# Router columns as weights in a ViT tower kernel: 512 positions stream, the logits are transposed afterwards

## The chip, the core and the metric

The kernel runs on one core of a Trainium2 chip. The metric is the device time of one execution in microseconds (us), from the first to the last instruction with what lies around it. Five engines work side by side: PE (TensorE, matrix products), DVE (VectorE), ACT (ScalarE), POOL (GpSimd) and SP (SyncE, which issues transfers). Each runs its own list in order and waits on semaphores for the others.

## What is computed

Four images pass through a tokenizer, a linear attention layer and a mixture of experts. Cut to what matters here:

```python
h = tokenizer(x)                        # sin and cos of 6 bands, 6912 features -> 192, 512 tokens per image
h = concat([cls_tok, h])
h = h + attention(layernorm(h))
x = layernorm(h)                        # input of the feed-forward part
probs = softmax(x @ router_w)           # 192 -> 8 experts
gates, idx = top_k(probs, 2)
gates = gates / sum(gates)
g = silu(einsum('bsd,edh->bseh', x, w_gate)); u = einsum('bsd,edh->bseh', x, w_up)
routed = sum over experts of dense_g * ((g * u) @ w_down)
shared = silu(x @ ws_gate) * (x @ ws_up) @ ws_down
alpha = sigmoid(x @ sg_w + sg_b)
out = h + alpha * shared + (1 - alpha) * routed
```

The router here is the product of the 192 features of a token with 10 columns: 8 experts, one column for alpha, one of zeros.

## The kernel before

Everything is in float32. Where exactness to float32 is wanted at the faster matmul format fp32r, an operand is split into a high part and a rest, and the products of the parts are summed in PSUM: high times high, high times rest, rest times high, and for the last 64 features (stacked twice, as `wrb`) two products.

The work has three stages. First come four records b = 0 to 3, one for each image. Each has nine projections `project(b, k)` of 24 matmuls (6 feature groups i times 4 blocks of 128 tokens), and the features of a projection are made beforehand by POOL (`rounds`), DVE (`remainders`) and ACT (`sines`, two of them). Between the projections stand the steps `attn1` to `attn8` of the attention of the record before; index a counts them, a = 0 for the class tokens and a = b for the image before record b. The second stage is the chunks q = 0 to 18 of the shared expert (`up(q)`: ten matmuls of 512 columns, `silu`, `hidden`, `down(q)`), between which the attention of the last image (a = 4) stands, and the splitting of the routed experts' weights into high part and rest (`expert_hi` on ACT, `expert_lo` on DVE). The third is 39 tiles of 128 routed rows, the remaining chunks and the sum.

All orders are written by hand, engine by engine; the numbers Q_... say at which chunk a step stands. The router runs five times. For a = 0 it stands between projections 7 and 8 of record 0; for a = 1 and 2 in records 2 and 3, behind `attn1(b)` and before `project(b, 1)`; for a = 3 before chunk 0; for a = 4 after chunk 11. On PE (L1430 to L1444) it takes, for each block of 128 tokens, the token features as weights (128 columns) and streams the 10 router columns, in five matmuls:

```python
o, c = ps[0:TP, logit_bank(a), 16 * i:16 * i + NR], slice(i * P, i * P + TP)
pe.matmul(o, xh_a_[:, c], wra_hi[:, :], start=True, stop=False)
```

The logits land with tokens on partitions, and DVE's `router(a)` copies them (L929) and picks the two best experts in a chain of some 14 short steps, then `ranks` on PE counts how many tokens each expert has, `places` on DVE works out the slots, and POOL scatters the tokens to them (`scatter`, L433). ACT's `router(a)` (L571) is one exponent for the gates, which DVE's `gates(a)` takes. SP loads the routed experts' weights (`raw_a`, `raw_b`) after the last projection, their down weights (`wd_ea`, `wd_eb`, L353 and L354) when all weights are split, and the first tiles `xs` (L363) when all tokens are scattered. `finish(f)` on DVE (L1044) empties the PSUM bank of the shared expert of an image; `down` of the next image's first chunk waits for it.

In records 2 and 3 the order on ACT is: `sines(b, 1)`, `sines(b, 2)`, `attn1(b)` (the copy `xt_a`, L496), `router(b - 1)`, `sines(b, 3)`.

## Time and profile before

| what | value |
|---|---|
| median of 3 runs | 570.83 us (570.6 to 571.26) |
| the profiled execution | 570.71 us |
| its span, first to last instruction | 568.9 us |
| mean granted clock of TensorE | 0.994 of full speed |
| DVE busy | 363.0 us (64%) |
| ACT busy | 245.9 us (43%) |
| POOL busy | 174.0 us (31%) |

The profile is one execution, recorded by the hardware. Its page gives busy times by engine, its other views the single instructions in order of time, what each engine waited for, and the clock that TensorE was granted. Matmul records overlap their neighbours, so the distance from start to start is what one costs, not the length of a record. A float32 matmul shows as two records, so 24 matmuls are x48; the fp32r ones and transposes show as one.

### The profile page before, as it was taken

Reading aid. Unit: us, or ns where it says so; the run is one execution under the profiler, and the core shown is the slowest. Engines: PE = TensorE matmul, PEld = TensorE weight load, DVE = VectorE, ACT = ScalarE, POOL = GpSimd, SP = SyncE. Lnnn points to the kernel's source line nnn. Section 1 sums busy time; section 2 is a strip of 40 time slices with the busy share of each in tenths; the row PEclk is TensorE's granted clock in tenths of the full one; section 3 lists DMA queues with packets and bytes.
Section 4 is the critical chain, followed back from the end, with each engine's and each line's share of the span. In section 5 each row is a group of like instructions: output and inputs, shape, how many; then the busy total and the mean of one; then the engine's idle time right before and its main releaser. Section 6 shows DMA issues by size and latency. Waiting matters only on the chain.

```text
span 568.9 us, 9027 instructions
## 1 busy us (share of the span) xinstructions
PE 555.4 (98%) x3247; PEld 510.8 (90%) x3247; DVE 363.0 (64%) x1040; ACT 245.9 (43%) x343; POOL 174.0 (31%) x200
## 2 busy tenths in 40 slices
PE   5999999999999999999999999999999999999997
PEld 5998999799999989999979899977888889999965
DVE  7736787532968736779761787376787546666537
ACT  3465364654225753442575523254224134545410
POOL 6413133122225311674311461001300504454410
PEclk9998999999999999999999999999998999999999
DMA  8900067000000000210000010330100561531164
GB/s 330 323 21 20 3 216 243 20 10 20 20 18 20 20 0 11 75 56 1 1 0 10 20 37 20 98 126 23 62 2 1 185 206 54 164 95 52 55 199 152
DMA packets 23487, 42.48 MB, mean 75 GB/s; under 512 B 2502, under 2 KB 15044, under 8 KB 23348
## 3 DMA queue, kind: packets, MB, share of 16 engines
q1 hardware_dynamic: 19560, 33.31, 18.1%
q0 software_dynamic: 3472, 8.07, 4.0%
q10 hardware_dynamic: 412, 0.53, 0.4%
q8 instruction: 27, 0.44, 0.3%
q14 instruction: 16, 0.13, 0.1%
HBM read 31.74 MB, written 14.79 MB: 82 GB/s over the span
## 4 chain that ended last, share of the span: by engine, by line
PE 90%; DVE 5%; ACT 3%; DMA 1%; issue 1%; POOL 0%; ACTq 0%; DVEq 0%
PE ps L1312 47%; PE ps L1505 4%; PE ps L1391 2%; PE ps L1557 2%; PE ps L1559 2%; PE ps L1467 2%; PE ps L1469 2%; PE ps L1470 2%; PE ps L1468 2%; PE ps L1471 2%; PE ps L1368 2%; PE ps L1535 1%; PE ps L1537 1%; PE ps L1536 1%; PE ps L1539 1%; PE ps L1538 1%
## 5 line engine op out<-in xcount | busy, mean ns | idle before, releaser
L1312 PE MATMUL ps<-w_tok,feat 128*128 128x192 f32 x1728 | 292.0, 330 | 7.5 <-ACT feat L469 6.3
L1312 PEld LDWEIGHTS ps<-w_tok,feat 128*128 128x128 f32 x1728 | 284.0, 192 | 11.0 <-issue 10.6
L403 POOL TENSOR_SCALAR feat<-fx 128x512 int32<-128x512 f32 x108 | 93.2, 878 | 204.7 <-PE ps L1312 201.3
L478 ACT ACTIVATE feat<-feat 128x1536 f32<-128x1536 f32 x35 | 51.9, 1484 | 118.6 <-DVE feat L773 116.0
L769 DVE SCALAR_TENSOR_TENSOR feat<-fx,feat 128x512 f32<-128x512 f32 x105 | 76.6, 782 | 1.9 <-POOL feat L403 1.5
L481 ACT ACTIVATE feat<-feat,half_pi 128x1536 f32<-128x1536 f32 x35 | 54.6, 1561 | 0.0
L439 POOL DMA_INDIRECT ydram<-yr,xs x39 | 37.4, 959 | 54.9 <-DVE yr L1085 54.9
L433 POOL DMA_INDIRECT slots<-pay_a,posi x17 | 18.4, 1082 | 74.2 <-DVE posi L1012 70.8
L773 DVE TENSOR_SCALAR feat<-feat 128x1536 int32<-128x1536 int32 x35 | 37.5, 1070 | 1.2
L1505 PE MATMUL ps<-w_down,hid_ring 128*128 128x192 f32 x192 | 36.4, 334 | 0.8 <-issue 0.4
L585 ACT ACTIVATE s_ring<-ps 128x512 f32<-128x512 f32 x24 | 14.4, 599 | 52.1 <-PE ps L1471 52.1
L1505 PEld LDWEIGHTS ps<-w_down,hid_ring 128*128 128x128 f32 x192 | 32.1, 192 | 3.0 <-issue 1.7
L1036 DVE TENSOR_TENSOR hid_ring<-s_ring,ps 128x512 f32<-128x512 f32 x24 | 16.4, 685 | 18.6 <-PE ps L1471 15.7
L607 ACT ACTIVATE xhr<-ps 128x256 fp32r<-128x256 f32 x39 | 15.0, 384 | 22.6 <-PE ps L1518 22.6
L1078 DVE TENSOR_TENSOR hidt<-sr,ps 128x192 f32<-128x192 f32 x39 | 13.8, 353 | 15.7 <-ACT sr L613 14.1
L1071 DVE TENSOR_TENSOR xlr<-ps,xhr 128x256 fp32r<-128x256 f32 x39 | 16.5, 424 | 10.6 <-ACT xhr L607 10.6
L817 DVE TENSOR_TENSOR_SCAN r<-one,s_c,r 128x512 f32<-128x512 f32 x4 | 5.1, 1284 | 27.4 <-ACT r L523 27.4
L1467 PE MATMUL ps<-X,wa_hi 128*128 128x512 f32 x48 | 22.3, 465 | 0.2 <-ACT s_ring L585 0.2
L1085 DVE TENSOR_SCALAR yr<-ps,xs 128x192 f32<-128x192 f32 x39 | 16.3, 418 | 8.6 <-PE ps L1559 8.0
L613 ACT ACTIVATE sr<-ps 128x192 f32<-128x192 f32 x39 | 12.9, 330 | 20.2 <-issue 15.4
L1557 PE MATMUL ps<-wd_ea,htr 128*128 x78 | 19.2, 328 | 0.7 <-DVE yr L1085 0.7
L1470 PE MATMUL ps<-X,wb 128*128 128x512 f32 x48 | 19.2, 400 | 0.0
(277 smaller groups left out, 857.2 us busy)
## 6 DMA issues: line engine op xcount, KB each, us to landing
slots<-in_blank SPq DMA_DIRECT2D x1, 5031.0 KB, 18.7
w_tok<-in_wT SPq DMA_DIRECT2D x7, 576.0 KB, 8.8
fx<-in_xT SPq DMA_DIRECT2D x15, 256.0 KB, 2.7
xs<-slots SPq DMA_DIRECT2D x5, 645.0 KB, 6.9
yin<-ydram SPq DMA_DIRECT2D x8, 384.0 KB, 7.2
raw_a<-in_wea SPq DMA_DIRECT2D x4, 384.0 KB, 5.1
raw_b<-in_web SPq DMA_DIRECT2D x4, 384.0 KB, 5.9
w_tok<-in_wT SPq DMA_DIRECT2D x4, 288.0 KB, 7.6
```

What stands on the lines that cost most here:

```text
L403: ins = pool.tensor_scalar(feat[:, k % SLOTS, i, :].bitcast(I32), x[:, x_block(k), :], f_col[:, fi:fi + 1], 1.0, ALU.mult, ALU.mult)
L433: pool.indirect_dma_start(slots, bass.IndirectOffsetOnAxis(ap=idx, axis=0), (pay_a[a % 2], pay_b)[c][0:TP, t, :], None).then_inc(scat, 16)
L439: pool.indirect_dma_start(ydram, bass.IndirectOffsetOnAxis(ap=idx, axis=0), yr[:, s % NYR, :], None).then_inc(yscat[s % NYR], 16)
L478: act.activation(feat[:, k % SLOTS, 0:3, :], feat[:, k % SLOTS, 0:3, :], ACT.Sin, scale=TWO_PI).then_inc(sin_ready, 1)
L481: act.activation(feat[:, k % SLOTS, 3:6, :], feat[:, k % SLOTS, 3:6, :], ACT.Sin, bias=half_pi[:, :], scale=-TWO_PI).then_inc(sin_ready, 1)
L769: ins = dve.scalar_tensor_tensor(feat[:, s, i, :], x[:, x_block(k), :], f_col[:, fi:fi + 1], feat[:, s, i, :].bitcast(I32), ALU.mult, ALU. ...
L773: dve.tensor_scalar(feat[:, s, 3:6, :].bitcast(I32), feat[:, s, 0:3, :].bitcast(I32), 0x7FFFFFFF, None, ALU.bitwise_and).then_inc(r_ready, 1)
L1312: ins = pe.matmul(ps[:, TOK[a % 2][t // 2], (t % 2) * D:(t % 2 + 1) * D], feat[:, k % SLOTS, i, t * P:(t + 1) * P], w_tok[:, k, i, :], sta ...
L1467: pe.matmul(o, wa_hi[:, c, i, :], xh, start=True, stop=False)
L1470: pe.matmul(o, wb[:, c, i, :], yh, start=False, stop=False)
L1505: ins = pe.matmul(ps[:, DN0 + t // 2, (t % 2) * D:(t % 2 + 1) * D], hid_ring[:, q % 3, t * P:(t + 1) * P], w_down[:, c, :], start=(c == 0 ...
L1557: pe.matmul(o, htr[:, s % 2, 0:P], wd_ea[:, bass.ds(e, 1), :].rearrange("p e n -> p (e n)"), start=True, stop=False)
```

## The change

The operands of the router change sides. The router's columns become the weights, high part and rest side by side in one tile `wra` of 20 columns (and `wrb` of 10), and 512 token positions stream past them: four matmuls in place of twenty, with the logits transposed in PSUM, 20 rows by 512. ACT copies them to SBUF (`take_lt`, into the new tile `lt`), PE transposes them back block by block (`router_rows`), and DVE's first step adds the two halves instead of copying.

On PE `router_rows` stands later than `router`: in records 2 and 3 after the first sixth of `project(b, 1)`, in record 0 after half of `project(0, 8)`, for a = 3 after `up(0)`, for a = 4 after `down(9)`. On ACT `take_lt(b - 1)` stands behind `attn1(b)`, and the exponent of `router(b - 1)` moves behind `sines(b, 3)`.

The split of the routed weights goes from quarters to eighths and stands at chunks 4, 4, 4, 7, 7, 9, 10, 10 on ACT (5, 5, 5, 8, 8, 10, 11, 11 on DVE) where it stood at 4, 7, 10, 13 (5, 8, 11, 14). Their loading stays in quarters.

```diff
-EP = 4
+EL = 4
+EP = 8
-Q_HI = (4, 7, 10, 13)
-Q_LO = (5, 8, 11, 14)
+Q_HI = (4, 4, 4, 7, 7, 9, 10, 10)
+Q_LO = (5, 5, 5, 8, 8, 10, 11, 11)
...
-        wra_hi, wra_lo, wrb = (sb(n, [P, NR], F32R) for n in ("wra_hi", "wra_lo", "wrb"))
+        wra, wrb = sb("wra", [P, 2 * NR], F32R), sb("wrb", [P, NR], F32R)
+        lt = sb("lt", [2 * NR, T])
...
+            def take_lt(a):
+                W, TP, nt = width(a)
+                act.wait_ge(lt_psum, a + 1)
+                act.activation(lt[:, 0:W], ps[0:2 * NR, logit_bank(a), 0:W], ACT.Copy).then_inc(lt_ready, 1)
...
             sines(0, 8)
+            take_lt(0)
             sines(1, 0)
...
                 attn1(b)
                 if b >= 2:
+                    take_lt(b - 1)
+                sines(b, 3)
+                if b >= 2:
                     router(b - 1)
-                sines(b, 3)
...
+            take_lt(B - 1)
             for q in range(NQB):
...
                 if q == Q_LG:
+                    take_lt(B)
                     router(B)
...
-                next_(dve.tensor_copy(lg[0:TP, 0:nt, :], ps[0:TP, logit_bank(a), 0:16 * nt].rearrange(
-                    "p (t n) -> p t n", n=16)[:, :, 0:NE + 1]))
+                halves = ps[0:TP, logit_bank(a), 0:32 * nt].rearrange("p (t c) -> p t c", c=32)[:, :, 0:2 * NR]
+                next_(dve.tensor_reduce(lg[0:TP, 0:nt, :], halves.rearrange("p t (h n) -> p t n h", h=2)[:, :, 0:NE + 1, :],
+                                        AX_X, ALU.add))
...
+                o = ps[0:2 * NR, logit_bank(a), 0:W]
+                pe.matmul(o, wra[:, :], xh_a_, start=True, stop=False, skip_group_check=True)
+                pe.matmul(o, wra[:, :], xl_a_, start=False, stop=False, skip_group_check=True)
+                pe.matmul(o[0:NR], wrb[:, :], xh_b_, start=False, stop=False, skip_group_check=True)
+                pe.matmul(o[0:NR], wrb[:, :], xl_b_, start=False, stop=True, skip_group_check=True).then_inc(lt_psum, 1)
+
+            def router_rows(a):
+                W, TP, nt = width(a)
+                pe.wait_ge(lt_ready, a + 1)
                 for i in range(nt):
...
+                    ins = pe.transpose(ps[0:TP, logit_bank(a), 32 * i:32 * i + 2 * NR], lt[:, i * P:i * P + TP],
+                                       ident[0:2 * NR, 0:2 * NR])
                 ins.then_inc(lg_psum, 1)
...
             router(0)
-            project(0, 8)
+            project(0, 8, range(3))
+            router_rows(0)
+            project(0, 8, range(3, 6))
...
                     router(b - 1)
-                project(b, 1)
+                project(b, 1, range(1))
+                if b >= 2:
+                    router_rows(b - 1)
+                project(b, 1, range(1, 6))
...
                 up(q)
+                if q == 0:
+                    router_rows(B - 1)
...
                     down(q - 2)
+                if q == Q_LG:
+                    router_rows(B)
```

How the rows stand on PE in record 2, around the router of a = 1, before (`xn` is the normalized input of the attention, `X` the split tokens, `feat` and `w_tok` the features and weights of the projection):

```order
L1323 MATMUL ps<-pack,xn 128x128 x4
L1325 MATMUL ps<-pack,xn 64x128 x4
L1439 MATMUL ps<-wra_hi,X 128x10
L1440 MATMUL ps<-wra_lo,X 128x10
L1441 MATMUL ps<-wra_hi,X 128x10
L1442 MATMUL ps<-wrb,X 128x10
L1443 MATMUL ps<-wrb,X 128x10
...
L1312 MATMUL ps<-w_tok,feat 128x192 x24
L1349 MATMUL ps<-xt_a,pack 128x512
```

The five router rows stand four times. The same place on PE after the change:

```order
L1339 MATMUL ps<-pack,xn 128x128 x4
L1341 MATMUL ps<-pack,xn 64x128 x4
L1456 MATMUL ps<-X,wra 20x512
L1457 MATMUL ps<-X,wra 20x512
L1458 MATMUL ps<-X,wrb 10x512
L1459 MATMUL ps<-X,wrb 10x512
L1327 MATMUL ps<-w_tok,feat 128x192 x4
L1465 MATMUL ps<-pack,lt 128x20 x4
L1327 MATMUL ps<-w_tok,feat 128x192 x20
L1365 MATMUL ps<-xt_a,pack 128x512
```

Four wide rows replace the twenty, and the transposes stand behind 4 of the projection's 24 matmuls. On ACT in the same record, from `sines(2, 2)` on, before:

```order
L478 ACTIVATE feat<-feat 128x1536
L481 ACTIVATE feat<-feat,half_pi 128x1536
L496 ACTIVATE xt_a<-ps 128x512
L571 ACT_TABLE_LOAD
L571 ACTIVATE ez<-dz 128x8
L478 ACT_TABLE_LOAD
L478 ACTIVATE feat<-feat 128x1536
L481 ACTIVATE feat<-feat,half_pi 128x1536
L515 ACT_TABLE_LOAD
L515 ACTIVATE r<-ps,pack 128x512
```

The first two rows are `sines(2, 2)`, the seventh and eighth `sines(2, 3)`. And after the change:

```order
L480 ACTIVATE feat<-feat 128x1536
L483 ACTIVATE feat<-feat,half_pi 128x1536
L498 ACTIVATE xt_a<-ps 128x512
L573 ACTIVATE lt<-ps 20x512
L480 ACTIVATE feat<-feat 128x1536
L483 ACTIVATE feat<-feat,half_pi 128x1536
L578 ACT_TABLE_LOAD
L578 ACTIVATE ez<-dz 128x8
L517 ACTIVATE r<-ps,pack 128x512
```

The copy `lt` stands behind `xt_a`, the exponent behind `sines(2, 3)`, and two loads of a function table are gone. On DVE at chunks 10 and 11, before (`X` is the split of the last image's tokens, L929 the start of its router):

```order
L909 TENSOR_TENSOR X<-ps,X 128x512
L910 TENSOR_TENSOR X<-ps,X 128x512
L1036 TENSOR_TENSOR hid_ring<-s_ring,ps 128x512
L1060 TENSOR_TENSOR e_lo<-raw_a,e_hi 128x768
L1064 TENSOR_TENSOR e_b<-raw_b,e_b 64x768
L929 COPY lg<-ps 128x36
```

And after the change:

```order
L1074 TENSOR_TENSOR e_lo<-raw_a,e_hi 128x384
L1078 TENSOR_TENSOR e_b<-raw_b,e_b 64x384
L922 TENSOR_TENSOR X<-ps,X 128x512
L923 TENSOR_TENSOR X<-ps,X 128x512
L1050 TENSOR_TENSOR hid_ring<-s_ring,ps 128x512
L1074 TENSOR_TENSOR e_lo<-raw_a,e_hi 128x384
L1078 TENSOR_TENSOR e_b<-raw_b,e_b 64x384
L1074 TENSOR_TENSOR e_lo<-raw_a,e_hi 128x384
L1078 TENSOR_TENSOR e_b<-raw_b,e_b 64x384
L943 TENSOR_REDUCE lg<-ps 128x36
```

The same amount of split stands ahead of the router's first step, one more eighth ahead of the token split.

## Rows read from the trace of the kernel before

**Rows 1.** The page, busy time by engine: us, share of the span, instructions.
```profile
PE 555.4 (98%) x3247; PEld 510.8 (90%) x3247; DVE 363.0 (64%) x1040; ACT 245.9 (43%) x343; POOL 174.0 (31%) x200
```

**Rows 2.** What PE waited for: total us, times, longest.
```profile
PE ps L1312 <- ACT feat L469: 6.3, 1, 6.3
```

**Rows 3.** Timeline of PE, records 2 and 3: start, us, work (copies).
```profile
186.78 0.25 PE L1439 MATMUL ps<-wra_hi,X 128*128 128x10 f32 x1
...
189.01 8.05 PE L1312 MATMUL ps<-w_tok,feat 128*128 128x192 f32 x48
196.90 0.59 PE L1349 MATMUL ps<-xt_a,pack 128*128 128x512 f32 x1
...
282.07 8.05 PE L1312 MATMUL ps<-w_tok,feat 128*128 128x192 f32 x48
```

**Rows 4.** Timeline of ACT, records 2 and 3; in brackets the idle time before.
```profile
187.91 1.48 ACT L478 ACTIVATE feat<-feat 128x1536 f32<-128x1536 f32 x1 [5.81 <-DVE feat L773]
189.30 1.56 ACT L481 ACTIVATE feat<-feat,half_pi 128x1536 f32<-128x1536 f32 x1
190.76 0.57 ACT L496 ACTIVATE xt_a<-ps 128x512 f32<-128x512 f32 x1
...
283.83 0.58 ACT L496 ACTIVATE xt_a<-ps 128x512 f32<-128x512 f32 x1
```

**Rows 5.** Timeline of DVE, before record 1 and in record 2.
```profile
88.53 1.14 DVE L739 BATCH_NORM_STATS2 st<-H 128x6 f32<-128x192 f32 x4 [2.42 <-ACT H L489]
...
92.50 1.25 DVE L755 TENSOR_SCALAR xn<-H,mv,y 128x192 f32<-128x192 f32 x4
...
200.92 0.69 DVE L804 TENSOR_SCALAR r<-ps 128x512 f32<-128x512 f32 x1 [4.71 <-PE ps L1352]
```

**Rows 6.** Timeline of PE, start of record 1.
```profile
95.23 0.60 PE L1323 MATMUL ps<-pack,xn 128*128 128x128 f32 x4
```

**Rows 7.** Timeline of PE near the end: two-column weights with 512 streaming, small transposes.
```profile
545.94 0.39 PE L1577 MATMUL ps<-wb,xc 128*2 128x512 f32 x1
546.17 0.40 PE L1467 MATMUL ps<-X,wa_hi 128*128 128x512 f32 x1
...
549.90 0.53 PE L1582 MATMUL ps<-pack,v 2*128 2x2 f32 x6
```

**Rows 8.** Timeline of PE, record 0: little work, a wait, a projection.
```profile
34.14 8.07 PE L1312 MATMUL ps<-w_tok,feat 128*128 128x192 f32 x48
...
42.86 0.48 PE L1391 MATMUL ps<-v,r 2*2 2x193 f32 x2
44.41 9.72 PE L1312 MATMUL ps<-w_tok,feat 128*128 128x192 f32 x48 [1.07 <-ACT feat L478]
```

**Rows 9.** Stretches: PE, PEld, DVE, ACT, POOL busy (instructions), PEclk, DMA, GB/s.
```profile
44.40:46.00 1.60, 1.59 (x6) 1.60 (x7) 1.33 (x9) 1.33 (x1) 0.24 (x1) 0.61 0.04 10
...
429.80:432.00 2.20, 2.20 (x11) 2.20 (x11) 1.94 (x8) 0.00 (x0) 0.00 (x0) 0.65 0.00 0
```

**Rows 10.** Timeline of PE, shared-expert chunks 1 to 12.
```profile
371.22 0.60 PE L1323 MATMUL ps<-pack,xn 128*128 128x128 f32 x4
...
429.83 2.31 PE L1505 MATMUL ps<-w_down,hid_ring 128*128 128x192 f32 x8
...
442.70 1.46 PE L1505 MATMUL ps<-w_down,hid_ring 128*128 128x192 f32 x8
```

**Rows 11.** Timeline of DVE, layer norm, weight split, router chain, finish.
```profile
369.39 1.25 DVE L755 TENSOR_SCALAR xn<-H,mv,y 128x192 f32<-128x192 f32 x4
...
398.13 0.95 DVE L1064 TENSOR_TENSOR e_b<-raw_b,e_b 64x768 fp32r<-64x768 f32 x1
400.93 0.23 DVE L859 TENSOR_SCALAR den<-ps 128x2 f32<-128x2 f32 x2 [1.85 <-PE ps L1391]
...
430.44 0.20 DVE L929 COPY lg<-ps 128x36 f32<-128x36 f32 x1
...
440.76 1.39 DVE L1044 SCALAR_TENSOR_TENSOR H<-ps,alpha,H 128x192 f32<-128x192 f32 x4
```

More of the change, by code:

```diff
@@ L201, in build @@
             xpose2 nta_ready ntb_ready wo_psum h2_ready xn2_ready xpose3 xh_ready xl_ready
-            lg_psum top_step dz_ready ez_ready gt_step oh_ready gates_ready rank_psum rk_ready pos_step slots_ready emap_ready
+            lt_psum lt_ready lg_psum top_step dz_ready ez_ready gt_step oh_ready gates_ready rank_psum rk_ready pos_step slots_ready emap_ready
             payb_ready scat
@@ L215, in build @@
          xpose2, nta_ready, ntb_ready, wo_psum, h2_ready, xn2_ready, xpose3, xh_ready, xl_ready,
-         lg_psum, top_step, dz_ready, ez_ready, gt_step, oh_ready, gates_ready, rank_psum, rk_ready, pos_step, slots_ready, emap_ready,
+         lt_psum, lt_ready, lg_psum, top_step, dz_ready, ez_ready, gt_step, oh_ready, gates_ready, rank_psum, rk_ready, pos_step, slots_ready, emap_ready,
          payb_ready, scat,
@@ L346, in _ @@
             sp.wait_ge(tok_group, NG * B)
-            for p in range(EP):
-                cut = slice(p * NE // EP, (p + 1) * NE // EP)
+            for p in range(EL):
+                cut = slice(p * NE // EL, (p + 1) * NE // EL)
                 cols = slice(cut.start * 2 * D, cut.stop * 2 * D)
@@ L595, in expert_hi @@
             def expert_hi(p):
-                act.wait_ge(eraw_in, 32 * EP)
+                act.wait_ge(eraw_in, 32 * EL)
                 cut = slice(p * NE // EP, (p + 1) * NE // EP)
@@ L703, in _ @@
                     take_ranks(B)
-                if q in Q_HI:
-                    expert_hi(Q_HI.index(q))
+                for p in range(EP):
+                    if Q_HI[p] == q:
+                        expert_hi(p)
             for i in range(NTILE + 2):
@@ L1148, in _ @@
             attn1(0)
-            dve.tensor_copy(wra_hi[:, :], wr_raw[:, 0, :])
+            dve.tensor_copy(wra[:, 0:NR], wr_raw[:, 0, :])
             dve.tensor_copy(wrb[:, :], wr_raw[:, 1, :]).then_inc(router_split, 1)
             dve.wait_ge(router_split, 1)
-            dve.tensor_tensor(wra_lo[:, :], wr_raw[:, 0, :], wra_hi[:, :].bitcast(F32), ALU.subtract)
+            dve.tensor_tensor(wra[:, NR:2 * NR], wr_raw[:, 0, :], wra[:, 0:NR].bitcast(F32), ALU.subtract)
             dve.tensor_tensor(wrb[DB:P, :], wr_raw[DB:P, 1, :], wrb[DB:P, :].bitcast(F32),
@@ L1248, in _ @@
                     places(B, [2])
-                if q in Q_LO:
-                    expert_lo(Q_LO.index(q))
+                for p in range(EP):
+                    if Q_LO[p] == q:
+                        expert_lo(p)
             dve.memset(hidt[:, :, D:2 * P], 0.0).then_inc(hidt_zero, 1)
@@ L1291, in _, with project @@
         def _(pe):
-            def project(a, k):
+            def project(a, k, recs=range(6)):
                 q = NG * a + k
@@ L1300, in project @@
                     pe.wait_ge(h_ready, a - 1)
-                for i in range(6):
+                for i in recs:
                     if q == 0 and i < 2:
@@ L1315, in project @@
                                         skip_group_check=True)
-                ins.then_inc(tok_group, 1)
+                if 5 in recs:
+                    ins.then_inc(tok_group, 1)
             def attn1(a):
@@ L1436, in router @@
                     pe.wait_ge(dz_ready, a)
-                for i in range(nt):
-                    o, c = ps[0:TP, logit_bank(a), 16 * i:16 * i + NR], slice(i * P, i * P + TP)
-                    pe.matmul(o, xh_a_[:, c], wra_hi[:, :], start=True, stop=False)
-                    pe.matmul(o, xh_a_[:, c], wra_lo[:, :], start=False, stop=False)
-                    pe.matmul(o, xl_a_[:, c], wra_hi[:, :], start=False, stop=False)
-                    pe.matmul(o, xh_b_[:, c], wrb[:, :], start=False, stop=False)
-                    ins = pe.matmul(o, xl_b_[:, c], wrb[:, :], start=False, stop=True)
+                if a >= 2:
+                    pe.wait_ge(rk_ready, a - 1)
+                o = ps[0:2 * NR, logit_bank(a), 0:W]
[6 more added lines that the diff above has]
+                pe.wait_ge(lt_ready, a + 1)
+                for i in range(nt):
+                    ins = pe.transpose(ps[0:TP, logit_bank(a), 32 * i:32 * i + 2 * NR], lt[:, i * P:i * P + TP],
+                                       ident[0:2 * NR, 0:2 * NR])
                 ins.then_inc(lg_psum, 1)
```

## The prediction

> **What bounds the kernel now.** I read the busy times by engine first: PE is busy 555.4 us of a span of 568.9 us [rows 1]. Then the list of what PE waited for: its longest entry, 6.3 us, is the start, before the first features exist [rows 2]. So nearly every microsecond that the change adds to PE's stream, or makes PE wait in it, is a microsecond of the span, and the other engines matter where PE waits for them. The timelines then show the places that the change touches: records 2 and 3 of the tokenizer, and the shared-expert chunks that run beside the last record's attention.
>
> In record 2 PE starts the router at 186.78 and the next projection at 189.01, and that projection's successor starts at 196.90 [rows 3]. Record 3 is the same 93.06 us later (282.07 for 189.01). What the reader must see beside it is ACT: at 187.91 and 189.30 it begins two sines of 1.5 us each, whose input DVE had just delivered, and only at 190.76 the copy xt_a, done at 191.33; in record 3 at 283.83 [rows 4]. ACT is thus more than 2 us behind PE's router here. Nobody minds before, since PE needs xt_a only at 196.90.
>
> **The router's arithmetic.** Now 20 matmuls with 10 streaming columns take 189.01 - 186.78 = 2.23 us, 0.11 us each, although they stream almost nothing: the 128-column weight load sets that pace. After, four matmuls stream 512 columns. The nearest rows are the class-token products, two-column weights with 512 streaming: 545.94 to 546.17, 0.23 us each [rows 7]. Four are 0.93 us. The four transposes that follow have no exact row. Six small transposes take 0.53 us [rows 7], 0.09 us each, so 0.35 us for four; at the old router's 0.11 us they would be 0.45 us, and I take that end, since the new ones load 128 columns as the router did. A router then costs 1.38 us, 0.85 us less (0.95 us with the lower end). Four routers have this form, so the work saved is 3.4 us. The router of the class tokens (two columns) stays near zero.
>
> **Does the narrow output cost a change of array mode?** The rows say no: the last two-column product starts at 545.94 and the next matmul, with 128 weight columns, 0.23 us later, the pace of the stream [rows 7]. The Trainium skill (TensorEngine Tiling, Key Properties) says that changing the tiling mode drains TensorE, which speaks against outputs of 20 and 10 columns if they switched it; by the 0.39 us that a product lasts against its 0.23 us pace, an estimate of that page's drain would be 0.16 us at each end of a router, 1.3 us for four. The trace shows none at the same kind of boundary, so I add nothing.
>
> **The wait that the change adds.** The new copy take_lt stands on ACT behind both sines and xt_a. It begins when xt_a is done, 191.33, and takes what a 512-column copy takes, 0.57 us [rows 4]: the logits are in SBUF at 191.90. PE meanwhile does the four wide matmuls from 186.78, to 187.71, and the first sixth of the projection. Its 24 matmuls took 196.90 - 189.01 = 7.89 us [rows 3], 0.33 us each, so four take 1.31 us and PE arrives at the transposes at 189.02. It waits there 2.9 us. Behind the transposes are queued the other 20 matmuls of the projection (6.58 us) and everything else on PE. The successor starts at 191.90 + 0.45 + 6.58 = 198.93 instead of 196.90: 2.0 us later. With the cheaper transposes and copies that overlap slightly it is 1.85 us; I take 1.95 us. Record 3 has the same distances (ACT 283.83, PE 282.07), so again 1.95 us. **Two records: +3.9 us.** PE waits for nothing else in these records, so nothing takes it up later.
>
> What hangs on the late logits? DVE's router starts 3.3 us later and ACT's exponent now comes behind the next two sines. DVE gates before it takes the keys at 200.92, where it had waited 4.71 us [rows 5]. The logits are 3.3 us late, the two sines cost 3.0 us [rows 4], an exponent's table load and the rest about as much as before; of these 6.3 us, 4.71 us are slack and 1.95 us come from PE's own delay. PE takes the result of this chain only after a whole further projection, 7.9 us. I price it at nothing; without that cover it would be an overrun of up to 1 us per record.
>
> In record 0 the transposes stand after 12 of 24 matmuls, 3.9 us, and ACT has no queue there, so PE does not wait. DVE's first router moves 3.9 us back, of which 2.42 us are idle [rows 5]; the layer norm ends at 93.75 + 1.5 = 95.25 against PE's need at 95.23 [rows 6]. That is 0 to 0.3 us; I take 0.
>
> **The clock.** Twice in the run the granted clock falls to its lower level, 1.2 GHz, in a stretch: the mean is 0.61 from 44.40 to 46.00 and 0.65 from 429.80 to 432.00 [rows 9]. The first follows 2.2 us, from 34.14 + 8.07 = 42.21 to 44.41, of tiny matmuls and a wait of 1.07 us, and the projection behind it lasts 9.72 us instead of 8.07: 1.65 us [rows 8]. The second follows the last router's 20 ten-column matmuls, about 2.2 us, that end at 429.83 [rows 10]. The same router in records 2 and 3 does not bring it down. The new stretch there is 2.9 us of pure wait and 0.45 us of thin transposes, longer and emptier than either that did. So each of the two new waits brings the clock down more likely than not; I take one of the two, **+1.65 us**, with zero and two as the bounds.
>
> **The chunk stage.** The router of record 3 now precedes chunk 0, its transposes follow it, and ACT has copied the logits long before that. PE gains 0.85 us, but the transposes L1323 that started at 371.22 [rows 10] need DVE's layer norm, which ends at 369.39 + 1.25 = 370.64 [rows 11] whatever PE does. **Gain 0.55 us.**
>
> The router after chunk 11 gains 0.85 us, and its ten-column stretch is gone, so the fall of the clock behind it (2.31 us for a down of 1.46 us, and more behind it [rows 10]) goes too: 1.65 us. But most of both is not kept. DVE's chain, router, gates, places and finish, starts at 430.44 behind its weight split and ends with the finish at 440.76 + 1.39 = 442.15 [rows 11], for reasons on DVE and ACT, and the down of chunk 12 needs that finish; it starts at 442.70 now [rows 10]. PE can start it at 442.2. **Gain 0.5 us**, and a new wait of about 2 us for DVE.
>
> The expert weights are split in eighths, three of them at chunk 5. A quarter's second half takes 0.95 us [rows 11], so a third eighth adds 0.95 us on DVE, inside the 1.85 us that DVE sits idle before it divides at 400.93 [rows 11]. ACT's extra copies delay the silu by some 0.9 us, which eats 0.3 us more. Nothing added; without cover it would be up to 0.5 us, since PE waits on this chain. Done by chunk 11, the splits let SP load the down weights before the scatters rather than beside them, which helps the first slot tiles but no wait of PE that the trace shows: 0.
>
> **The sum.** 3.9 + 1.65 - 0.55 - 0.5 = +4.5 us. The profiled execution took 570.71 us (span 568.9 us), close to the median of 570.83 us. 570.7 + 4.5 = **575.2 us**, slower.
>
> **The rivals.**
> - The same, and the clock does not fall at the new waits: 573.5 us. For it: the routers of records 2 and 3 last 2.2 us at ten columns, with no fall. Chance 0.24.
> - The same, and it falls at both: 576.8 us. Chance 0.22.
> - The chunk stage keeps all it saves: if DVE's chain came 2 us earlier, the other 0.3 + 2.0 us would be kept, 572.9 us with one fall and 571.2 with none. Against: DVE has hardly a gap from 430.44 to 442.15. Chance 0.08, half of it without a fall and within 0.2%.
> - Faster: the logits come in time. It decides at a copy that is done by 189.0 and not 191.9, which asks that ACT begin its sines 2.9 us earlier, or that PE finds the rows later. Then each record gives 0.85 us back and the time is 570.7 - 1.7 - 1.05 = 568.0 us. Against: ACT waited for DVE until 187.91, and nothing before that moves. Chance 0.05.
> - Drains or an overrun of DVE on top, 577 us and more, the page's estimate among them (576.5 with one fall). Chance 0.05.
> - The forecast: 0.36.
>
> The range from 572.8 to 577.1 holds the first three and half of the chunk rival. About 0.2%, 1.1 us, is what a measurement can tell from no change. Faster 0.05, same 0.04, slower 0.91.
>
> **What would show it.** Right: PE waits for ACT's lt copy twice, 2.9 us each, in records 2 and 3; four wide router matmuls 0.23 us apart; no low clock behind the last router, but one behind a wait; PE waiting for DVE's finish at the down of chunk 12. Wrong: an lt copy that starts before xt_a, transposes far from 0.11 us each, or a wait of PE behind the first projection of record 2 that is not there now.

## The result and the profile after

The changed kernel takes **579.39 us** (median; 576.92 to 579.95, 4 runs) against 571.0 us (570.6 to 571.26, 4 runs) for the kernel before: 1.0131 times as long, interval 1.0106 to 1.0155. (The ratios here and below are estimates from all the runs of both kernels, each with a 95% interval, and differ slightly from the quotient of the two medians, here 1.0147.) The forecast was 575.2 us with a range of 572.8 to 577.1 us. The direction came out as said, the size did not: +8.4 us in place of +4.5 us. The profiled execution is the one of 579.39 us; its span is 577.4 us, 8.5 us over the span of before, so the sum can be made up between the two traces. In the batches below, the runs of one kernel lie in groups some 2.5 us apart (the kernel before at 568, 571 and 573.5 us, besides one run of 722 us at a granted clock of 0.749, which is left out of the ratio), so ratios and medians are taken over the runs of a whole batch, and single profiles are compared stretch by stretch.

The busy times by engine of the page, to be read beside [rows 1]: PE is 1.2 us longer busy although the change took 48 records and some 3 us of work from it, and its share fell from 98% to 96%.

```profile
PE 556.6 (96%) x3199; PEld 508.0 (88%) x3199; DVE 363.9 (63%) x1048; ACT 243.6 (42%) x352; POOL 176.1 (30%) x200
```

What PE waited for (us in total, times, longest), to be read beside [rows 2]:

```profile
PE ps L1327 <- ACT feat L471: 6.3, 1, 6.3
PE ps L1465 <- ACT lt L573: 5.2, 2, 2.6
PE ps L1528 <- DVE H L1058: 1.6, 2, 1.1
...
PE ps L1477 <- DVE oh L957: 0.8, 1, 0.8
```

The second line is the wait that the change adds, twice 2.6 us. The third and the last are in the chunk stage: the wait for `finish`, and the one for the one-hot rows `oh` from which `ranks` counts. The timeline of PE in records 2 and 3 (start, us, in brackets the idle time before), beside [rows 3]:

```profile
187.39 0.48 PE L1456 MATMUL ps<-X,wra 128*20 128x512 f32 x1
...
188.41 1.46 PE L1327 MATMUL ps<-w_tok,feat 128*128 128x192 f32 x8
192.47 0.61 PE L1465 MATMUL ps<-pack,lt 20*128 20x20 f32 x4 [2.60 <-ACT lt L573]
193.01 9.67 PE L1327 MATMUL ps<-w_tok,feat 128*128 128x192 f32 x40
202.52 1.02 PE L1365 MATMUL ps<-xt_a,pack 128*128 128x512 f32 x2
...
290.79 0.42 PE L1465 MATMUL ps<-pack,lt 20*128 20x20 f32 x4 [2.62 <-ACT lt L573]
291.14 8.41 PE L1327 MATMUL ps<-w_tok,feat 128*128 128x192 f32 x40
299.39 1.02 PE L1365 MATMUL ps<-xt_a,pack 128*128 128x512 f32 x2
```

The same 40 records behind the transposes last 9.67 us once and 8.41 us the other time; at full clock they last 6.77 us (a row of the first experiment shows it). That is where the forecast's missing microseconds are. ACT in record 2, beside [rows 4]:

```profile
188.51 1.48 ACT L480 ACTIVATE feat<-feat 128x1536 f32<-128x1536 f32 x1 [5.81 <-DVE feat L786]
189.90 1.56 ACT L483 ACTIVATE feat<-feat,half_pi 128x1536 f32<-128x1536 f32 x1
191.37 0.58 ACT L498 ACTIVATE xt_a<-ps 128x512 f32<-128x512 f32 x1
191.84 0.57 ACT L573 ACTIVATE lt<-ps 20x512 f32<-20x512 f32 x1
```

ACT stands idle for 5.81 us ahead of the sines, takes both and `xt_a`, and only then the copy for which PE waits. The stretches (PE, PEld, DVE, ACT, POOL busy with instructions, then the granted clock, DMA share, GB/s), beside [rows 9]:

```profile
180.00:192.14 12.14, 9.87 (x62) 9.07 (x60) 8.64 (x29) 6.33 (x6) 3.92 (x5) 1.00 0.04 17
192.14:199.00 6.86, 6.53 (x23) 6.49 (x24) 5.43 (x19) 0.27 (x1) 0.00 (x0) 0.50 0.00 0
...
291.05:294.45 3.40, 3.40 (x13) 3.37 (x12) 2.79 (x16) 0.00 (x0) 0.00 (x0) 0.51 0.00 0
...
430.00:440.00 10.00, 10.00 (x55) 7.97 (x54) 8.57 (x21) 5.69 (x10) 1.65 (x3) 1.00 0.00 0
440.00:450.00 10.00, 9.17 (x52) 7.51 (x51) 7.72 (x45) 3.15 (x6) 0.00 (x0) 1.00 0.43 157
```

The clock goes to the lower level, 1.2 GHz, at 192.14, just before the end of the first wait, while PE is still idle, and stays there 6.86 us. After the second wait, which ends at 290.79, it falls at 291.05 and stays there 3.40 us. Behind the last router, where it fell before [rows 9], it stays at 2.4 GHz.

The difference of the two spans, cut at the starts of the same instructions (before: 79.28 for the first row of record 0's router, 95.23 [rows 6], 186.78 and 196.90 [rows 3], and the last two again 93.06 us later):

| stretch | before | after | difference |
|---|---|---|---|
| start to the router of record 0 | 79.28 | 79.60 | +0.3 |
| that router to record 1's transposes | 15.95 | 16.23 | +0.3 |
| from there to record 2's router | 91.55 | 91.56 | 0.0 |
| record 2, router to the projection's successor | 10.12 | 15.13 | +5.0 |
| from there to record 3's router | 82.94 | 83.19 | +0.25 |
| record 3, the same two places | 10.12 | 13.68 | +3.56 |
| from there to the end | 278.94 | 278.01 | -0.9 |

The first +0.3 us lie before anything that the change touches.

### The profile page after: what moved, and what is told of

Its sections match the earlier page's. It is cut to its first block, busy times and chain, and to the rows that moved or that the text cites. A ratio compares the mean times of both kernels' runs of the same rounds, so it can differ in the third digit from the quotient of the medians.

```text
span 577.4 us, 8952 instructions
## 1 busy us (share of the span) xinstructions
PE 556.6 (96%) x3199; PEld 508.0 (88%) x3199; DVE 363.9 (63%) x1048; ACT 243.6 (42%) x352; POOL 176.1 (30%) x200
## 4 chain that ended last, share of the span: by engine, by line
PE 79%; DVE 12%; ACT 6%; issue 1%; DMA 1%; POOL 0%; ACTq 0%; DVEq 0%
PE ps L1327 42%; PE ps L1528 3%; PE ps L1580 2%; PE ps L1582 2%; PE ps L1407 2%; PE ps L1384 2%; DVE feat L782 1%; PE ps L1490 1%; PE ps L1558 1%; PE ps L1494 1%; PE ps L1492 1%; PE ps L1493 1%; PE ps L1491 1%; PE ps L1559 1%; PE ps L1561 1%
## 5 line engine op out<-in xcount | busy, mean ns | idle before, releaser
L1327 PE MATMUL ps<-w_tok,feat 128*128 128x192 f32 x1728 | 297.4, 334 | 7.6 <-ACT feat L471 6.3
L1327 PEld LDWEIGHTS ps<-w_tok,feat 128*128 128x128 f32 x1728 | 288.8, 195 | 11.5 <-issue 10.6
L405 POOL TENSOR_SCALAR feat<-fx 128x512 int32<-128x512 f32 x108 | 94.8, 892 | 212.5 <-PE ps L1327 209.0
L1582 PE MATMUL ps<-wd_eb,htr 128*128 x78 | 19.1, 326 | 0.0
```

The lines of the kernel that those rows point to most:

```text
L405: ins = pool.tensor_scalar(feat[:, k % SLOTS, i, :].bitcast(I32), x[:, x_block(k), :], f_col[:, fi:fi + 1], 1.0, ALU.mult, ALU.mult)
L1327: ins = pe.matmul(ps[:, TOK[a % 2][t // 2], (t % 2) * D:(t % 2 + 1) * D], feat[:, k % SLOTS, i, t * P:(t + 1) * P], w_tok[:, k, i, :], sta ...
L1582: pe.matmul(o, htr[:, s % 2, P:2 * P], wd_eb[:, bass.ds(e, 1), :].rearrange("p e n -> p (e n)"), start=False, stop=True).then_inc(rdn_psum, 1)
```

## The experiments

The theory after the result (A): ACT's order makes the wait, since the copy stands behind the two sines and `xt_a`; PE's idle time makes the clock fall; and late logits as such cost nothing. The rivals: the transposes or the narrow outputs cost time themselves; the clock falls for another reason than the wait, such as the thin work around it; and the chain behind the late logits (DVE, ACT) costs part of it.

### The copy first on ACT

```diff
                 sines(b, 1)
+                if b >= 2:
+                    take_lt(b - 1)
                 sines(b, 2)
                 attn1(b)
-                if b >= 2:
-                    take_lt(b - 1)
```

> The changed kernel with one move: in records 2 and 3 ACT takes the logits (take_lt) before sines(b, 2) instead of behind attn1. Theory A (ACT's place of the copy causes the waits, and the waits bring the clock down): both waits of 2.6 us go, and with them the low clock behind them, which cost 3.1 and 1.8 us; 579.4 - 5.2 - 4.9 = 569.3 us, one and a half us under the kernel before (571.0). Theory B (the clock falls because the new router and its transposes are thin work, whoever waits): the waits go, the low clock stays: 574.2 us. Theory C (the late DVE chain is what costs): the logits come 3 us sooner, the time falls by less than 5 us.

Measured: 568.92 us (566.91 to 569.48, 10 runs), 0.9961 times the kernel before, interval 0.9935 to 0.9987. ACT's timeline in record 2, then PE's:

```profile
188.64 0.59 ACT L573 ACTIVATE lt<-ps 20x512 f32<-20x512 f32 x1 [5.90 <-PE ps L1459]
```
```profile
189.83 0.42 PE L1465 MATMUL ps<-pack,lt 20*128 20x20 f32 x4
190.18 6.77 PE L1327 MATMUL ps<-w_tok,feat 128*128 128x192 f32 x40
196.78 1.02 PE L1365 MATMUL ps<-xt_a,pack 128*128 128x512 f32 x2
```

One line moved on ACT gives 10.5 us back. Between the two profiled spans it is 577.4 - 567.2 = 10.2 us, and that is made up of 5.2 us of waiting, 4.7 us of the clock (worked out below) and 0.2 us that PE waited for the transfer of `r`. The copy now runs in ACT's idle time, PE reaches the transposes 1.39 us after it has begun the projection (at 188.44) and finds the logits ready, no wait for `lt` is in its list, and the 40 records last 6.77 us. From the router, which starts at 187.42, to the successor PE takes 196.78 - 187.42 = 9.36 us in place of 10.12 us before: 0.76 us less, where the forecast's arithmetic said 0.85 us. So the new form of the router is cheaper, and everything that the change cost in these records came from the place of one copy.

### The wait filled with work

```diff
                 if b >= 2:
+                    for _ in range(8):
+                        pe.matmul(ps[:, A2, 0:D], feat[:, 1, 0, 0:P], w_tok[:, 1, 0, :], start=True, stop=True,
+                                  skip_group_check=True)
                     router_rows(b - 1)
```

Nothing is left out of the computation; the eight products go to a bank that is overwritten later and are used by nobody.

> The changed kernel with eight more float32 matmuls of 192 columns on PE (written to a free bank and used by nobody) ahead of the transposes in records 2 and 3, 2.6 us that fill the wait for ACT's copy. Theory A: the transposes start when they did, PE is busy instead of waiting, so the clock stays up and only that part comes back: 579.4 - 4.9 = 574.5 us. Theory B: the clock falls all the same: 579.4 us or a little more.

Measured: 574.32 us (571.75 to 575.03, 10 runs), ratio 1.0041, interval 1.0012 to 1.007. That is 5.1 us less than the changed kernel, with 5.5 us more work on PE. The rows of record 2:

```profile
187.09 2.76 PE L1649 MATMUL ps<-w_tok,feat 128*128 128x192 f32 x16
...
190.21 6.77 PE L1327 MATMUL ps<-w_tok,feat 128*128 128x192 f32 x40
```

The filler lasts about as long as the wait did (2.76 us for 2.60 us), the transposes start as late, and the 40 records are back at 6.77 us with the granted clock at 1.00. This separates the two costs of a wait: the time itself, and the clock behind it. The second is what the 5.1 us are, against 9.67 + 8.41 - 2 x 6.77 = 4.5 us in the rows of the two projections, and 0.2 us in the slower transposes of record 2.

### The kernel before with the wait alone

```diff
                 if b >= 2:
                     router(b - 1)
+                    pe.wait_ge(xta_ready, b + 1)
                 project(b, 1)
```

> The kernel before with nothing but a wait: in records 2 and 3 PE waits, behind the old router and ahead of project(b, 1), until ACT has copied xt_a (it needs that copy only a projection later). From the trace of before the copy is done at 191.33 and PE arrives at 189.01, so 2.3 us of waiting each, 4.6 us. Theory A: the wait also brings the clock down, at least once in each record, 1.7 us each: 571.0 + 4.6 + 3.4 = 579.0 us, more where the low clock lasts twice as long. Theory B (a wait of this length does not touch the clock): 575.6 us.

Measured: 582.37 us (576.38, then four runs from 581.55 to 582.54), ratio 1.0198, interval 1.0138 to 1.0258. The profile is of the lowest run. From its list of waits:

```profile
PE ps L1312 <- ACT xt_a L496: 4.5, 2, 2.2
```

From its timeline of PE, in record 2 and in record 3:

```profile
189.02 9.75 PE L1312 MATMUL ps<-w_tok,feat 128*128 128x192 f32 x48 [2.24 <-ACT xt_a L496]
```
```profile
286.17 9.48 PE L1312 MATMUL ps<-w_tok,feat 128*128 128x192 f32 x48 [2.24 <-ACT xt_a L496]
```

And the stretches around both, with the granted clock as the third number from the right:

```profile
190.00:200.00 10.00, 10.00 (x47) 9.09 (x46) 3.72 (x11) 6.00 (x6) 1.13 (x2) 0.83 0.12 28
280.00:290.00 10.00, 7.76 (x49) 7.65 (x48) 8.89 (x24) 6.21 (x6) 2.84 (x3) 0.83 0.01 2
```

Without wide matmuls or transposes, 4.5 us of waiting bring the clock down behind both waits (the twenty ten-column matmuls ahead of each stand there in the kernel before too, where no fall followed them): 9.75 and 9.48 us for the 8.05 us of [rows 3], 1.70 and 1.43 us. Each of the two is about what the forecast took for one fall (1.65 us). So two waits alone explain 4.5 + 3.1 = 7.6 us. The typical run of this kernel is 11.0 us slower than the typical run of before, which is 3.4 us more. It has no trace, so whether a low stretch of the double length, as in record 2 of the changed kernel, is in it stays open.

### The split alone

The kernel before with the eighths and their places at chunks 4, 4, 4, 7, 7, 9, 10, 10 and the router as it was.

```diff
-EP = 4
-Q_HI = (4, 7, 10, 13)
-Q_LO = (5, 8, 11, 14)
+EL = 4
+EP = 8
+Q_HI = (4, 4, 4, 7, 7, 9, 10, 10)
+Q_LO = (5, 5, 5, 8, 8, 10, 11, 11)
```

> The kernel before with only the second half of the change: the expert weights split in eighths at chunks 4, 4, 4, 7, 7, 9, 10, 10 (5, 5, 5, 8, 8, 10, 11, 11 on DVE). The forecast priced this at 0: 571.0 us, within 0.3. Rival: the third eighth at chunk 5 delays DVE's divide and PE behind it, up to 0.5 us: 571.5 us.

Measured: 570.88 us (570.25 to 573.33), ratio 0.9995, interval 0.9968 to 1.0022. The forecast's zero for the split holds for the whole, but the trace shows small effects of both signs under it. From the transposes of chunk 0 to the last router PE takes 56.64 us in place of 56.46 us. And a wait of PE ahead of the `down` at the first slot tile, which starts at 459.32 in the kernel before, is gone here and in the changed kernel; in the list of before it is

```profile
PE ps L1505 <- issue: 0.4, 1, 0.4
```

Beside these, DVE's router behind chunk 11 starts 3.11 us after PE's and not 2.76 us, since the split ahead of it is now four short steps in place of two (2.31 us for 1.95 us). PE does not wait for that in this kernel; in the changed one it does.

### The transposes later: after 8 of 24 matmuls

```diff
-                project(b, 1, range(1))
+                project(b, 1, range(2))
                 if b >= 2:
                     router_rows(b - 1)
-                project(b, 1, range(1, 6))
+                project(b, 1, range(2, 6))
```

> The changed kernel with the transposes of records 2 and 3 behind 8 of the projection's 24 matmuls instead of 4, so that PE arrives 1.3 us later and waits 1.3 us instead of 2.6. The waits themselves give back 2.6 us. Theory A1 (how far the clock falls depends on how long PE is empty): it mostly stays up, 579.4 - 2.6 - 4.9 = 571.9 us. Theory A2 (any wait on top of thin work is enough): it falls at least once in each record, 579.4 - 2.6 - 1.5 = 575.3 us.

Measured: 571.96 us (571.23 to 572.46, 10 runs), ratio 0.9996, interval 0.9978 to 1.0014. The list of waits has

```profile
PE ps L1465 <- ACT lt L573: 2.6, 2, 1.3
```

twice 1.3 us, and the rows behind them are at full pace (5.47 us for 32 records, the same as 6.77 us for 40). Each wait was halved by 1.30 us, and with the clock that did not fall the kernel got 7.4 us faster: 2.6 us from waiting, 4.8 us from the clock.

### The transposes after 16 of 24 matmuls

The same edit with `range(4)` and `range(4, 6)`. PE arrives after the copy, so A expected the same as with the copy first.

> The changed kernel with the transposes of records 2 and 3 behind 16 of the 24 matmuls, 3.9 us later on PE; ACT's order is untouched. PE arrives at about 193.6 with the logits ready at 192.4, so both waits go, as in the first experiment, but the logits reach DVE later still. Theory A (only PE's wait and the clock behind it cost): 569.3 us, the same as with the copy moved on ACT (568.9). Theory C (DVE's chain behind the logits costs): it is slower than that by the delay of DVE beyond its slack, 1 us or more in each record, 571 us.

Measured: **583.63 us** (583.23 to 584.68), ratio 1.02, interval 1.016 to 1.0239. It is the slowest kernel of all. Theory C had the kind of cost, DVE's chain, but 571 us for it, 12.6 us too few. PE does not wait for the copy any more, but for a transfer some 30 us later. From its list of waits, then from its timeline of PE in record 2:

```profile
PE ps L1384 <- DMA r<-r: 6.9, 2, 3.5
```
```profile
193.51 0.42 PE L1465 MATMUL ps<-pack,lt 20*128 20x20 f32 x4
...
223.18 4.63 PE L1384 MATMUL ps<-r 64*128 64x512 f32 x8 [3.41 <-DMA r<-r]
```

The transfer of `r` is the end of a chain over DVE and ACT: remainders of projection 3, sines of projection 3, exponent and keys, running sum, transfer. The forecast had priced its delay at nothing and named the cover. This kernel's timelines of DVE, ACT and POOL, one after the other:

```profile
193.97 0.23 DVE L943 TENSOR_REDUCE lg<-ps 128x36 f32<-128x72 f32 x1 [4.95 <-PE ps L1465]
...
197.03 3.30 DVE L782 SCALAR_TENSOR_TENSOR feat<-fx,feat 128x512 f32<-128x512 f32 x3
```
```profile
201.36 1.48 ACT L480 ACTIVATE feat<-feat 128x1536 f32<-128x1536 f32 x1 [9.12 <-DVE feat L786]
...
220.90 0.47 ACTq L536 DMA_DIRECT2D r<-r  x1
```
```profile
196.82 2.97 POOL L405 TENSOR_SCALAR feat<-fx 128x512 int32<-128x512 f32 x3 [7.30 <-PE ps L1327]
```

With the copy first the remainders start at 193.35 and take 2.07 us, the sines start at 196.45, and the transfer is issued at 217.68. Here DVE works off the router's chain first, and the remainders start 3.7 us later. They then run beside POOL's rounding and take 3.30 us, and POOL's takes 2.97 us for 2.02 us. The sines are 4.9 us late, the transfer 3.2 us, and PE waits 3.41 us. The clock falls as well: the eight records take 4.63 us for 2.42 us.

Two causes were left for this delay: DVE's order (the remainders behind the router's chain) and ACT's (the exponent, moved behind the sines by the change). The next two kernels put one of them right each.

### Transposes after 16, the exponent back ahead of the sines

```diff
+                if b >= 2:
+                    router(b - 1)
                 sines(b, 3)
-                if b >= 2:
-                    router(b - 1)
```

> The kernel with the transposes behind 16 of 24 matmuls, with one thing put back: in records 2 and 3 ACT takes the router's exponent before the two sines of projection 3, as in the kernel before. Theory A (DVE's own order is the cause: the router's chain, 3.1 us from the logits at 193.97, stands ahead of the remainders of projection 3, so these start at 197.03 instead of 193.35, and ACT's sines at 201.36 instead of about 196.4, wherever the exponent stands): ACT has 9.12 us of idle time ahead of these sines, so the exponent costs nothing there; what it gives back is only the gates' 0.95 us and the wait for them ahead of DVE's L817, about 1.1 us in each record. PE still waits for the transfer of r, about 2.3 us twice in place of 3.4 us, and the time is 581.4 us, or 579 us if the granted clock falls behind one of these waits less. Theory B (the exponent's place behind the sines is the cause): the waits for r go, and the time is 569 to 570 us.

Measured: 577.46 us (576.26 to 577.96, 4 runs), ratio 1.0107, interval 1.0055 to 1.0159. From its list of waits, then from ACT's timeline in record 2:

```profile
PE ps L1384 <- DMA r<-r: 3.5, 2, 1.8
```
```profile
197.95 0.21 ACT L578 ACTIVATE ez<-dz 128x8 f32<-128x8 f32 x1 [3.61 <-DVE dz L960]
```

The exponent is free here, ACT waits for DVE anyway, and each wait of PE is 1.7 us shorter (1.1 us were expected). So the exponent's place is half of the wait, 6.2 us of the time with the clock; the other half is still there, and the exponent is not the whole cause. It gives back more than its own time, since behind a shorter wait the eight records last 2.93 us and not 4.63 us.

### Transposes after 16, the remainders ahead of the router on DVE

```diff
                 attn1(b)
-                if b >= 2:
-                    router(b - 1)
                 remainders(b, 3)
                 if b >= 2:
+                    router(b - 1)
                     gates(b - 1)
```

> The kernel with the transposes behind 16 of 24 matmuls, and in records 2 and 3 DVE makes the remainders of projection 3 before the router's chain instead of behind it; the exponent stays behind the sines. Theory A (the remainders behind the late chain are the cause): the remainders start at about 190 to 193 us as soon as POOL has rounded, the sines of projection 3 at about 196.5, the exponent at about 200.7 as in the kernel with the copy put first, PE waits neither for lt nor for r, and the time is 568.9 to 569.5 us, the same as with the copy put first. Theory B (the exponent's place behind the sines, or the lateness of the logits as such): the waits for r stay at 2 us or more in each record, and the time is 578 us or more.

Measured: 568.67 us (566.55 to 569.74, 10 runs), ratio 0.996, interval 0.9935 to 0.9985, 15 us less than the kernel with the transposes at the same place on PE. Its list of waits has, for the transfer,

```profile
PE ps L1383 <- DMA r<-r: 0.2, 1, 0.2
```

and ACT's timeline in record 2:

```profile
190.18 1.48 ACT L480 ACTIVATE feat<-feat 128x1536 f32<-128x1536 f32 x1 [0.42 <-DVE feat L786]
...
194.66 0.21 ACT L578 ACTIVATE ez<-dz 128x8 f32<-128x8 f32 x1 [0.23 <-DVE dz L960]
```

The sines no longer wait for the router's chain, the exponent keeps its place behind them, and the wait for `r` is down to 0.2 us in one record, although the logits come as late behind PE's router as in the slow kernel (6.77 us). With DVE's order right, neither the late logits nor the exponent's place costs anything more; DVE's order is what made the lateness expensive.

### Record 0: the transpose earlier

The copy first, and in `project(0, 8)` the transpose after 4 of 24 matmuls in place of 12.

```diff
-            project(0, 8, range(3))
+            project(0, 8, range(1))
             router_rows(0)
-            project(0, 8, range(3, 6))
+            project(0, 8, range(1, 6))
```

> The first experiment's kernel (logits taken before the sines) with the transpose of record 0 behind 4 of the projection's 24 matmuls instead of 12, so that DVE's first router starts 2.6 us sooner. In the trace of the changed kernel record 1 begins 0.3 us later against the projection than before, behind a layer norm that DVE ended at 95.15 + something. Theory: that 0.3 us comes back, 568.6 us against 568.9. Rival: the 0.3 us was noise of PE's start, nothing changes.

Measured: 568.72 us (566.6 to 569.95, 8 runs), ratio 0.9948, interval 0.992 to 0.9977: no different from the copy first. In both kernels PE goes from the first matmul of `project(0, 8)` to the next record's transposes without a wait, in 95.86 - 79.87 = 15.99 us with the copy first and 93.38 - 77.40 = 15.98 us here, against 15.69 us before ([rows 6] and 79.54). So the 0.3 us do not depend on when DVE gets the logits. They go with the break of the projection by one tiny transpose: 83.95 to 84.06 is 0.11 us for it, and most of the rest lies in the records ahead of it: 24 records in 83.95 - 79.87 = 4.08 us, where the pace of before ([rows 6] and 79.54, 96 records) gives 3.92 us. Why these are slower no run shows.

### The order in the chunk stage

On top of the last kernel: DVE takes `finish(1)` ahead of `hidden(13)` and places the second slots one chunk later, and PE takes `ranks` behind `down`.

```diff
-                if q in (NCS + 2, 2 * NCS + 2):
+                if q in (NCS + 2, 2 * NCS + 1):
                     finish(q // NCS - 1)
...
-                if q == Q_RK:
+                if q == Q_RK + 1:
                     places(B, [1])
...
-                if q == Q_RK:
-                    ranks(B)
                 if q >= 2:
                     down(q - 2)
+                if q == Q_RK:
+                    ranks(B)
```

> The kernel of the run before this one with DVE's finish of the second image ahead of places(B, [1]) and with PE's ranks(B) behind the down of chunk 10 instead of ahead of it. In the changed kernel PE waits 0.83 us for DVE's oh at the ranks and 1.09 us for the finish at the down of chunk 12. Theory (the router's gain at chunk 11 is lost to these two waits): both go, 568.6 - 1.9 = 566.7 us. Rival: the scatters come 2 us later and the first tiles with them, PE waits at the tile stage instead: 568.6 us. Rival: DVE's chain is as long as before and the next wait on it takes up half: 567.7 us.

Measured: 568.27 us (565.47 to 568.61, 7 runs), ratio 0.9932, interval 0.9907 to 0.9957. The waits in the stage fell as meant:

```profile
PE ps L1490 <- ACT s_ring L592: 0.7, 2, 0.4
PE ps L1528 <- DVE H L1058: 0.5, 1, 0.5
```

The wait for `oh` (0.8 us) is gone and the one for `finish` is 0.5 us once, not 1.6 us. Another, for `silu`, grew from 0.2 to 0.7 us. The two profiled spans differ by 564.8 - 563.4 = 1.4 us, the medians by 0.45 us, which their scatter does not tell from nothing. This is the fastest of the kernels by its median, and it beats both that were given; most of that is the copy's place.

## Why the prediction was right and wrong

**What bounds the kernel.** Right. Where the span grew most, by 5.0 and 3.56 us, PE waited and then ran at the lower clock.

**The router's arithmetic.** Right. The four wide matmuls stand 0.23 us apart at the last router (rows below); in record 2, behind transposes, the four take 1.02 us (187.39 to 188.41) in place of 0.93 us. The transposes are 0.35 us (290.79 to 291.14), the lower of the two ends. Together that is 1.37 us for 2.23 us, 0.86 us less, for the 0.85 us said. The whole was only 0.76 us cheaper, because the projection broken by the transposes lasts 1.39 + 6.60 = 7.99 us (188.44 to 189.83 and 190.18 to 196.78 with the copy first) in place of 7.89 us; the forecast had no term for these 0.10 us.

**A change of array mode.** The timeline of PE at the last router shows the steps from 128 to 20 and from 20 to 10 columns:

```profile
436.61 0.40 PE L1494 MATMUL ps<-X,wb 128*128 128x512 f32 x1
436.84 0.39 PE L1456 MATMUL ps<-X,wra 128*20 128x512 f32 x1
437.07 0.40 PE L1457 MATMUL ps<-X,wra 128*20 128x512 f32 x1
437.30 0.39 PE L1458 MATMUL ps<-X,wrb 128*10 128x512 f32 x1
437.53 0.40 PE L1459 MATMUL ps<-X,wrb 128*10 128x512 f32 x1
437.77 1.46 PE L1528 MATMUL ps<-w_down,hid_ring 128*128 128x192 f32 x8
```

The starts are 0.23 or 0.24 us apart at every boundary, the way back to 128 columns among them, so there was no drain. The Trainium skill (TensorEngine Tiling (Array Packing), Key Properties) says that a change of tiling mode drains TensorE; these narrow outputs, at any rate, did not bring one. (The forecast counts its estimate of drains, 576.5 us, with the rival of 577 us and more, though it lies below that.)

**The added wait.** Right in place, cause and size: 2.6 us in each record for 2.9 us. ACT's sines started 1.1 us behind PE's router (188.51 to 187.39) as before. Without the clock the records cost 5.01 - 2.90 - 0.19 = 1.92 us and 3.56 - 1.64 = 1.92 us, where 2.90 and 1.64 us are what the 40 records took over 6.77 us, and 0.19 us the transposes at the lower clock (0.54 for 0.35 us). The forecast was 1.95 us each. The gain from undoing it is 10.5 us, and the copy's place alone does it.

**The clock. This is the step that failed**, the term of +1.65 us. Two things in it were wrong. I took one fall of two; both waits had one in the trace of after and in that of the wait alone. And I took the price of a fall from record 0's row, 1.65 us, as if all were alike. The one in record 3 did cost 1.64 us, but that in record 2 lasted 6.86 us in place of 3.40 us and cost 3.09 us with its transposes. Together 4.73 us, over the upper bound of 3.3 us that I had given. The rival "it falls at both", 576.8 us, was nearer, and short by that second length. Filling the wait with work of no use is the direct proof: the transposes came as late, and the kernel took 5.1 us less. What the rows of before could have told: both falls there follow a stretch of 2.2 us, one of tiny products and 1.07 us of idle time, the other of thin matmuls without a gap; a stretch with 2.6 us of pure idle time lies outside what they cover, so the bound should have been open upwards.

**Record 0.** Taken as 0, bounds 0 to 0.3; measured 0.3 us, and for another reason than the layer norm that I had named: moving the transpose eight matmuls earlier changed nothing, so the logits' time is not it.

**The chain behind the late logits.** I priced it at nothing, and up to 1 us per record without cover. In the changed kernel it cost 0.22 us once, in front of L1384. The cover was PE's own delay: with the transposes later and PE no longer waiting for them, it became 3.4 us of waiting in each record plus the clock, 12.3 us over before. The bound was too small because I followed the exponent on ACT and not the steps queued behind the router's chain on DVE, above all the remainders for projection 3, and of the two kernels that put one of them right each, the one with the remainders ahead lost the whole wait and 15.0 us, the one with the exponent ahead half of it and 6.2 us. The remainders stand on DVE behind the instruction that waits for the logits, and I had not listed them.

**The chunk stage.** The total is right within 0.15 us, -0.93 us from record 3's successor to the end for the -1.05 us said, but the second half of it (0.5 us) is luck. Cut at the same instructions, the parts are:

| stretch | before | after | difference | said |
|---|---|---|---|---|
| record 3's successor to the transposes of chunk 0 | 81.26 | 80.76 | -0.50 | -0.55 |
| from there to the last router | 56.46 | 56.69 | +0.23 | 0 |
| last router to the `down` of chunk 12 | 15.02 | 15.02 | 0.00 | -0.5 |
| from there to the `down` of the first slot tile | 16.62 | 16.10 | -0.52 | 0 |
| from there to the end | 109.58 | 109.44 | -0.14 | 0 |

The last router's gain of 0.5 us did not come. DVE in the changed kernel, beside [rows 11]:

```profile
439.37 0.56 DVE L1078 TENSOR_TENSOR e_b<-raw_b,e_b 64x384 fp32r<-64x384 f32 x1
439.96 0.23 DVE L943 TENSOR_REDUCE lg<-ps 128x36 f32<-128x72 f32 x1
442.69 0.19 DVE L957 TENSOR_TENSOR oh<-oh 128x32 bf16<-128x32 f32 x1
450.33 1.39 DVE L1058 SCALAR_TENSOR_TENSOR H<-ps,alpha,H 128x192 f32<-128x192 f32 x4
```

The router's first step stands right behind the split as before, but 3.12 us behind PE's router instead of 2.76 us, as with the split alone, and `finish` ends 11.76 us after it (11.71 us before). That takes up the 0.41 us that PE stands closer to `finish` now (0.14 us behind it, 0.55 us before). The 0.52 us came from the wait at the first slot tile that the split removes, which the forecast had at nothing. PE in turn waits 0.83 us for `oh` and 1.09 us for `finish`, 1.9 us in all, for the "about 2 us" of the forecast. The clock behind the router stays up, as said.

**The split.** Right as a whole, 0.9995, with the small effects of both signs told above.

**The sum made again.** 2 x 1.92 + 4.73 + 0.3 (record 0) + 0.25 (before record 3, mostly the transfer of `r`) - 0.93 + 0.3 (the start) = +8.5 us. Of the miss of 4.0 us, the clock is 3.1 us.

## What to carry to other kernels

- When an engine's result has to pass through another engine and come back, look for where the copy between them can stand in that engine's idle time, and put it there, not behind work that arrives at the same moment: here the same operation two places earlier was worth 10.5 us.
- A wait of PE has two prices, its length and the clock behind it; take the second from rows only up to the idle time that those rows had, and leave the range open above.
- A wait can hide a second delay of the same source, so before moving the first away, list what stands in the queue behind the late step on every engine: here transposes moved later on PE alone made the kernel 4 us slower, and together with DVE's remainders moved ahead 2.6 us faster than before.

## What the runs showed of the hardware

- Two waits of 2.6 us each brought the granted clock to the lower level, one while PE was still idle and for 6.86 us, one 0.26 us after its end and for 3.40 us, although the wait and the work around it were the same. Waits of 2.24 us in the kernel before did too (projections of 9.75 and 9.48 us for 8.05 us). Waits of 1.3 us at the same two places, with dense projections on both sides, did not in the profiled run.
- POOL's rounding and DVE's remainders at the same time, both over 128x512 tiles, were slower than apart: POOL's three roundings 2.97 us for 2.02 us and DVE's three remainder steps 3.30 us for 2.07 us.
- The start alone moves a run by some 2.5 us: in two profiles with the same work the first 96 records lasted 18.43 and 17.45 us, and record 0's projection behind its 1.07 us wait kept the full clock in the second (48 records in 8.04 us) and not in the first or in [rows 8]. That fits the groups of run times, though it was seen in profiles only.
